# Attention setup and first value products as single pieces in the recurrences' last steps, and weighing as the last work of an attention step

## The chip, the cores and the metric

One core of one Trainium2 chip runs the whole program. The metric is the device time of one execution in microseconds (us), as the median of three runs; a further execution was taken by the hardware profiler. The engines are PE (TensorE, matrix products), DVE (VectorE), ACT (ScalarE), POOL (GpSimd) and SP (SyncE, which here only issues DMAs). Each has its own instruction stream, and they meet only at semaphores.

## The reference

Four residual layers over x of shape (8, 512, 512): batch B = 8, time T = 512, width D = 512.

```python
# layer 0: gated recurrence over time
fused = sigmoid(concat([x_t, h]) @ w_W + w_b); r, o = split(fused)
m = x_t @ wx_W + wx_b + r * (h @ wh_W + wh_b)
h = o * h + (1 - o) * tanh(m)
# layers 1 and 2: h = tanh(x_t @ Wx + b + h @ Wh)
# layer 3: causal attention, 16 heads of 32, with one more key and value, the "image" (from cond)
q, k, v = split(x @ c_attn_w + c_attn_b)
k = concat([cond @ uk_w.T + uk_b, k]); v = concat([cond @ uv_w.T + uv_b, v])
scores = where(causal, q @ k.T / sqrt(32), -10000.0) + mask
x = x + (softmax(scores) @ v) @ c_proj_w + c_proj_b
```

## The kernel before

**Three blocks in a row.** Between blocks stands a barrier of all engines that clears the semaphores (`clear_signals`). The first is the scan (`scan`) with all three recurrences as one software pipeline of 548 steps. Step n works on time n of layer 0, time n-18 of layer 1 and time n-36 of layer 2. So layer 0 ends with step 511; steps 512 to 529 hold layers 1 and 2 ("double steps" below), and steps 530 to 547 hold layer 2 alone ("single steps"). In such a step PE multiplies the last states by the recurrent weights (`main12`, L189), DVE transposes the product (L275) and adds the input part (L285), ACT takes the tanh (L238), and the next step's PE work waits for it. The input parts (`fills`, L208) of 16 times come in a few steps of every 16: in 512 to 515 and in 530 and 531 near the end. Every 16 steps DVE also adds finished states to the residual (`chunk_sum`, L321 and L323).

**The attention's setup** (`attention_setup`) is the second block. PE spreads two bias rows over partitions (L589), turns the two image weight matrices (L599, 32 transposes) and multiplies them by the condition (L605, L610); DVE and POOL keep the results and make constants. The DMAs of the attention's weights (uk, uv, proj, qkv; 6 MB) are issued in the scan, when layer 0 has ended (L156).

**The attention** (`attention`) is the third block: 128 steps, each a unit of one batch element, one group of 4 heads and one quarter of the queries (qc = 0 to 3). 16 steps make one batch element; l is the step's place in it. PE's order in step i is written out by hand: the scores of unit i (L753), two transposes of the weights of unit i-2 (L774, "rounds" into banks 4 and 5, which ACT copies out, L860), one projection job, the weighing of values for unit i-3 (`weigh`, L796 and L802), the other rounds of unit i-2 (L774, then the sums' round L779, L780), and the remaining jobs. Jobs are 128x512 products for k, q (L730), v (L719), the hidden part (L713, L715), the output projection (L736), and the turned residual rows (L726). All jobs share bank 6: a job waits until DVE has kept the job before (`product_kept`). The jobs are spread by a table: with two jobs in a step at l = 0 (k, v), 2 (hidden, rows), 5 (q, rows), 6 (proj, rows) and 9 (q, rows). Ahead of step 0 stand five products of batch element 0: k, q, v, v, v. DVE first makes the mask's parts (L976 to L1008), and only then keeps the k product (L907).

The last units' buffers for sums, maxima and shares are rings of 4 (`RING`).

Of the kernel before, what the change touches and what calls it, by code (L numbers as in the profile page):

```python
# [21 lines left out]
ALU = mybir.AluOpType  # L22
# [3 lines left out]
P = 128  # L26
B, T, D = 8, 512, 512
KC = D // P
# [50 lines left out]

def counts(per_step):  # L80
    out = [0]
    for n in range(STEPS + 1):
        out.append(out[-1] + per_step(n))
    return out
# [24 lines left out]
def scan(nc, mem, sems, a):  # L109
# [10 lines left out]
    tiles = TILES[EARLY:]  # L120

# [9 lines left out]
    with nc.Block(no_gpsimd_drain=True) as block:  # L131

        @block.sync
        def _(sp):
# [18 lines left out]

            sp.wait_ge(s.update_done, T)
            for dst, src in ((mem.uk_rows, a["uk_w"]), (mem.uv_rows, a["uv_w"]), (mem.w_proj, a["proj_w"]), (mem.w_qkv, a["qkv_w"])):
                sp.dma_start(dst[:, :, :], src.rearrange("(k p) n -> p k n", p=P)).then_inc(s.weights_in, 16)  # L156
            sp.wait_ge(s.weights_in, 64)

        @block.tensor
        def _(pe):  # L160
# [60 lines left out]

            for n in range(STEPS):
                if n < T:
                    main0(n)
                if layers_of(n):
                    main12(n)
                if fills_of(n):
                    fills(n)
                if tile_of(n) is not None:
                    turn_tile(tile_of(n))  # L230

        @block.scalar
        def _(act):
# [16 lines left out]
            for n in range(STEPS + 1):  # L250
# [15 lines left out]
                if n < T:  # L266
                    gates(n)

        @block.vector
        def _(dve):  # L270
# [92 lines left out]

            for n in range(STEPS + 1):
# [10 lines left out]
                if n < T:  # L375
                    step0(n)

# [122 lines left out]
HG = 4  # L500
HPG = 4
HD = P // HPG
QC = T // P
PER = HG * QC
UNITS = B * PER
EXTRAS = 2
FAR = 32
MASK_OUT = -10000.0
FAR_UP = 1.0e30
HIGHEST = 3.0e38  # L510
TRI = [0, 1 + P, 2 + 3 * P, 3 + 6 * P, 3 + 10 * P]
RING = 4


HEAD_START = [("k", 0), ("q", 0), ("v", 0), ("v", 1), ("v", 2)]
# [7 lines left out]
def jobs_of(i):  # L523
# [7 lines left out]
    if u + 1 < B and l in OF_NEXT:  # L531
        jobs += [(u + 1, *job) for job in OF_NEXT[l]]
# [9 lines left out]
def attention_setup(nc, mem, sems, a):  # L542


    s = sems
    ukT, uvT = mem.ukT, mem.uvT
    turns = [(rows, dst, o, k) for rows, dst in ((mem.uk_rows, ukT), (mem.uv_rows, uvT)) for k in range(KC) for o in range(KC)]
    NTURN = len(turns) // KC

    with nc.Block(no_gpsimd_drain=True) as block:  # L550

        @block.sync
        def _(sp):
            for q, src in enumerate((a["qkv_b"][2 * D:3 * D], a["proj_b"], a["uv_b"])):
                sp.dma_start(mem.row_biases[0:1, q, :], src.rearrange("(o n) -> o n", o=1)).then_inc(s.small_in, 16)

        @block.gpsimd
        def _(pool):
            nc.gpsimd.memset(mem.ones[0:1, :], 1.0).then_inc(s.ident, 1)
            nc.gpsimd.memset(mem.drop[:, :], -HIGHEST).then_inc(s.zeroed, 1)  # L560
            nc.gpsimd.memset(mem.pick[:, :, :], 0.0).then_inc(s.zeroed, 1)
            pool.wait_ge(s.zeroed, 2)


            nc.gpsimd.affine_select(out=mem.drop[:, :], in_=mem.drop[:, :],
                                    compare_op=ALU.is_ge, fill=FAR_UP, base=0,
                                    pattern=[[-1, P]], channel_multiplier=1).then_inc(s.zeroed, 1)
            for q in range(QC):
                ins = nc.gpsimd.memset(mem.pick[:, :, FAR * q + 1:FAR * q + EXTRAS * HPG:EXTRAS], 1.0)
            ins.then_inc(s.picked, 1)  # L570
            pool.wait_ge(s.picked, 1)
            nc.gpsimd.affine_select(out=mem.pick[:, :, :], in_=mem.pick[:, :, :],
                                    compare_op=ALU.is_ge, fill=0.0, base=0,
                                    pattern=[[-1, B], [0, P]], channel_multiplier=1).then_inc(s.picked, 1)
            pool.wait_ge(s.picked, 2)
            nc.gpsimd.affine_select(out=mem.pick[:, :, :], in_=mem.pick[:, :, :],
                                    compare_op=ALU.is_ge, fill=0.0, base=0,
                                    pattern=[[1, B], [0, P]], channel_multiplier=-1)
            nc.gpsimd.memset(mem.hidden_w[:, :, :], 0.0)
            nc.gpsimd.memset(mem.probs_extra[:, :, :], 0.0)  # L580
            nc.gpsimd.memset(mem.head_wide[:, :], 0.0).then_inc(s.head_wide, 1)
            nc.gpsimd.memset(mem.k_image[:, :, :, :], 0.0).then_inc(s.image_zero, 1)

        @block.tensor
        def _(pe):
            pe.wait_ge(s.ident, 1)
            pe.wait_ge(s.small_in, 48)
            for q in range(2):
                mm = pe.matmul(mem.banks[q][:, :], mem.ones[0:1, :], mem.row_biases[0:1, q, :],  # L589
                               start=True, stop=True)  # L590
            mm.then_inc(s.rows_made, 1)
            pe.wait_ge(s.head_wide, 2)
            pe.transpose(mem.banks[6][:, 0:P], mem.head_wide[:, :], mem.ident[:, :]).then_inc(s.head_turned, 1)
            for q in range(NTURN):
                if q >= 2:
                    pe.wait_ge(s.turn_kept, q - 1)
                for r in range(KC):
                    rows, dst, o, k = turns[q * KC + r]
                    mm = pe.transpose(mem.banks[2 + q % 2][:, o * P:(o + 1) * P],  # L599
                                      rows[:, o, k * P:(k + 1) * P], mem.ident[:, :])  # L600
                mm.then_inc(s.turned, 1)
            pe.wait_ge(s.turn_kept, NTURN)
            for o in range(KC):
                for k in range(KC):
                    pe.matmul(mem.banks[4][:, B * o:B * (o + 1)],  # L605
                              ukT[:, k, o * P:(o + 1) * P], mem.condT[:, k, :],
                              start=(k == 0), stop=(k == KC - 1))
            pe.matmul(mem.banks[5][0:B, :], mem.ones[0:1, 0:B], mem.row_biases[0:1, 2, :], start=True, stop=False)
            for k in range(KC):
                mm = pe.matmul(mem.banks[5][0:B, :], mem.condT[:, k, :], uvT[:, k, :],  # L610
                               start=False, stop=(k == KC - 1))
            mm.then_inc(s.image_made, 1)

        @block.vector
        def _(dve):

            dve.wait_ge(s.head_wide, 1)
            for g in range(HPG):
                mine = mem.head_wide[HD * g:HD * (g + 1), :].rearrange("p (q c) -> p q c", q=QC)
                ins = nc.vector.memset(mine[:, :, EXTRAS * g:EXTRAS * (g + 1)], 1.0)  # L620
            ins.then_inc(s.head_wide, 1)
            nc.vector.memset(mem.tail_sum[:, :, :], 0.0)
            nc.vector.memset(mem.neg_later[:, :, QC - 1:QC], HIGHEST)

            dve.wait_ge(s.head_turned, 1)
            nc.vector.tensor_copy(mem.head_block[:, :], mem.banks[6][:, 0:P])
            dve.wait_ge(s.rows_made, 1)
            for q in range(2):
                nc.vector.tensor_copy(mem.bias_tiles[:, q, :], mem.banks[q][:, :])
            for q in range(NTURN):  # L630
                dve.wait_ge(s.turned, q + 1)
                _, dst, _, k = turns[q * KC]
                nc.vector.tensor_copy(dst[:, k, :], mem.banks[2 + q % 2][:, :]).then_inc(s.turn_kept, 1)
            dve.wait_ge(s.image_made, 1)
            dve.wait_ge(s.image_zero, 1)

            for hg in range(HG):
                col = BIAS_AT["uk_b"] + hg
                nc.vector.tensor_scalar(mem.k_column[:, hg, :], mem.banks[4][:, B * hg:B * (hg + 1)],
                                        mem.biasT[:, col:col + 1], None, ALU.add)  # L640
                for g in range(HPG):
                    rows = slice(HD * g, HD * (g + 1))
                    nc.vector.tensor_scalar(mem.k_image[rows, :, hg, g], mem.banks[4][rows, B * hg:B * (hg + 1)],
                                            mem.biasT[rows, col:col + 1], None, ALU.add)
            nc.vector.tensor_copy(mem.v_rows[0:B, :], mem.banks[5][0:B, :])

            at = BIAS_AT["qkv_b"]
            nc.vector.tensor_scalar(mem.q_bias[:, :], mem.biasT[:, at:at + HG], -HD ** -0.5, None, ALU.mult)


def attention(nc, mem, sems, a, out):
# [26 lines left out]
    with nc.Block(no_gpsimd_drain=True) as block:  # L678
# [25 lines left out]
        def _(pe):  # L704
# [105 lines left out]
            for job in HEAD_START[2:]:  # L810
                product(0, *job)
            pe.wait_ge(s.image_kept, 1)
            for i in range(UNITS + 3):
# [11 lines left out]
                if i >= 3:  # L825
                    weigh(i - 3)
# [457 lines left out]
```

## Time and profile before

| | us |
|---|---|
| median of 3 runs | 3901.76 (3895.54 to 3902.09) |
| profiled execution, own time | 3889.26 |
| its span | 3887.5 |
| PE busy in the span | 3772.9 (97%) |
| DVE, ACT, POOL busy | 2362.2, 1101.2, 36.8 |

Busy time is the union of an engine's instructions. A fp32 matrix product is recorded as two instructions, so the product of one 128x512 job (4 products) shows as x8. Ends of matrix instructions are modelled, so the distance from start to start is the safer measure. The number in square brackets is idle time ahead of an instruction and what ended it. "issue" there means that the profile shows nothing that was waited for.

### The profile page before, as it was taken

The page shows a single profiled execution, that of the slowest core. Times are in us where ns is not written, and L with a number is a line of the kernel's source. Part 1 is how long each engine was busy: PE and PEld are TensorE (multiplying, and loading weights), DVE is VectorE, ACT ScalarE, POOL GpSimd, SP SyncE. Part 2 cuts the span into 40 slices and gives each one's busy share as a digit, 9 for nine tenths or more (in the row PEclk, how much of TensorE's full clock was granted, in tenths as well). Part 3 has the DMA queues.
Part 4 walks back from the last instruction along what each step waited for, and adds up shares of the span by engine and source line. Part 5 has one row for each costly group of instructions (what it writes and reads, how often), then busy time and mean ns, then how long its engine had stood idle before and what let it go on. Part 6 is the DMA issues. An engine that isn't in the chain of part 4 may idle for free. (4 is left out here: it accounts for less than half of the span.)

```text
span 3887.5 us, 170553 instructions
## 1 busy us (share of the span) xinstructions
PE 3772.9 (97%) x77572; PEld 2491.0 (64%) x77572; DVE 2362.2 (61%) x8931; ACT 1101.2 (28%) x3961; POOL 36.8 (1%) x181
## 2 busy tenths in 40 slices
PE   7999999999999999999999999999868999999998
PEld 5777666667776666677766666677534555555555
DVE  4566666666666666666666666666535666766665
ACT  2221111111111111111111111111104555655565
POOL 0000000000000000000000000000000000000000
PEclk9999999999999999999999999999979999999999
DMA  4100000000000000000000000000100000000000
GB/s 170 31 4 3 3 3 3 3 4 3 3 3 3 3 3 4 3 3 3 3 3 4 3 3 3 3 3 3 68 1 7 12 9 12 15 12 12 13 9 20
DMA packets 34249, 46.64 MB, mean 12 GB/s; under 512 B 5819, under 2 KB 22251, under 8 KB 33526
## 3 DMA queue, kind: packets, MB, share of 16 engines
q1 hardware_dynamic: 31222, 29.43, 2.4%
q8 instruction: 610, 9.99, 1.1%
q10 hardware_dynamic: 2304, 6.29, 0.4%
q14 instruction: 113, 0.93, 0.1%
HBM read 27.33 MB, written 8.39 MB: 9 GB/s over the span
## 5 line engine op out<-in xcount | busy, mean ns | idle before, releaser
L189 PE MATMUL bank<-wh,h 128*16 128x256 f32 (+1 forms) x16960 | 987.7, 374 | 32.3 <-ACT h L238 32.3
L167 PE MATMUL bank<-wh,h 128*8 128x256 f32 x16352 | 976.1, 379 | 9.0 <-DVE h L361 9.0
L189 PEld LDWEIGHTS bank<-wh,h 128*16 128x16 f32 (+1 forms) x16960 | 490.2, 97 | 339.6 <-ACT h L238 45.3
L167 PEld LDWEIGHTS bank<-wh,h 128*8 128x8 f32 x16352 | 444.8, 90 | 345.8 <-DVE h L361 20.0
L333 DVE STREAM_TRANSPOSE tp<-bank 128x256 f32<-128x256 f32 x512 | 230.2, 450 | 607.0 <-PE bank L167 605.3
L173 PE MATMUL bank<-wh,h 128*8 128x128 f32 x16352 | 540.0, 273 | 0.0
L173 PEld LDWEIGHTS bank<-wh,h 128*8 128x8 f32 x16352 | 447.1, 90 | 108.2
L243 ACT ACTIVATE gates_sb<-pre_sb 128x32 f32<-128x32 f32 x512 | 117.3, 229 | 1207.7 <-DVE pre_sb L335 1207.7
L208 PE MATMUL bank<-first,w_qkv 128*32 128x128 f32 x11904 | 393.1, 273 | 0.0
L208 PEld LDWEIGHTS bank<-first,w_qkv 128*32 128x32 f32 x11904 | 339.9, 110 | 64.3
L238 ACT ACTIVATE h<-sum 128x64 f32<-128x64 f32 (+1 forms) x530 | 135.0, 255 | 779.5 <-DVE sum L285 779.5
L275 DVE STREAM_TRANSPOSE tp<-bank 128x256 f32<-128x256 f32 (+1 forms) x530 | 233.4, 440 | 129.7 <-PE bank L189 62.5
L299 DVE TENSOR_SCALAR xw<-bank,biasT 128x128 f32<-128x128 f32 x628 | 208.1, 348 | 158.3 <-PE bank L208 124.3
L847 ACT ACTIVATE probs<-probs,neg_max 128x385 f32<-128x385 f32 (+3 forms) x512 | 280.1, 553 | 0.0
L860 ACT COPY probsT<-bank 128x512 f32<-128x512 f32 x320 | 175.0, 588 | 333.7 <-PE bank L774 333.7
L208 PE MATMUL bank<-stage,wx 128*32 128x128 f32 x8192 | 247.9, 273 | 2.2 <-issue 2.2
L208 PEld LDWEIGHTS bank<-stage,wx 128*32 128x32 f32 x8192 | 229.1, 110 | 24.8 <-issue 2.9
L730 PE MATMUL bank<-X,w_qkv 128*128 128x512 f32 x512 | 233.0, 598 | 10.0 <-PEq L100 6.5
L943 DVE CUSTOM_DVE_ANT_0 probs<-bank,addends 128x385 f32<-128x385 f32 (+3 forms) x512 | 217.8, 482 | 31.6 <-PE bank L753 30.4
L340 DVE STREAM_TRANSPOSE tp<-bank 128x128 f32<-128x128 f32 x512 | 162.3, 317 | 79.8 <-PE bank L173 74.2
L774 PE MATMUL bank<-ident,probs 128*128 128x128 f32 x1280 | 184.0, 283 | 8.0 <-ACT probs L847 6.7
L774 PEld LDWEIGHTS bank<-ident,probs 128*128 128x128 f32 x1280 | 137.4, 142 | 78.4 <-issue 55.1
(146 smaller groups left out, 3148.6 us busy)
## 6 DMA issues: line engine op xcount, KB each, us to landing
xrows<-in_x_dram SPq DMA_DIRECT2D x32, 256.0 KB, 2.9
out_dram<-X SPq DMA_DIRECT2D x32, 256.0 KB, 2.6
w_qkv<-in_L_cond_c_attn_w_dram SPq DMA_DIRECT2D x1, 3072.0 KB, 17.7
w_qkv<-in_L_cond_w_W_dram ACTq DMA_DIRECT2D x4, 512.0 KB, 7.6
wh<-in_L_cond_w_W_dram ACTq DMA_DIRECT2D x4, 512.0 KB, 13.4
wx<-in_L_cond_Wx_dram SPq DMA_DIRECT2D x2, 1024.0 KB, 7.2
wh<-in_L_cond_Wh_dram SPq DMA_DIRECT2D x2, 1024.0 KB, 10.0
mask_all<-in_mask_Bx1x1xS_ff_dram SPq DMA_DIRECT2D x8, 256.0 KB, 3.2
```

What stands on the lines that cost most here:

```text
L167: mm = pe.matmul(mem.ps0[32 * j:32 * j + B, 0:2 * P], state[:, k, :], columns_of(mem.wh0[:, k, 0:3:2, :], j), start=(k == 0), stop=(k == K ...
L173: mm = pe.matmul(mem.ps0o[32 * j:32 * j + B, 0:P], state[:, k, :], columns_of(mem.wh0[:, k, 1:2, :], j), start=(k == 0), stop=(k == KC - 1))
L189: mm = pe.matmul(mem.ps12[32 * j:32 * j + B * len(ls), P * l0:P * l1], h12[:, k, (n - 1) % HR, l0:l1, :].rearrange("p l b -> p (l b)"), co ...
L208: mm = pe.matmul(mem.fillps[n % 2][32 * j:32 * (j + 1), f * N:(f + 1) * N], mem.wx[layer][:, k, at:at + 32], rows, start=(k == 0), stop=(k ...
L275: nc.vector.transpose(mem.tp12[:, P * l0:P * l1], mem.ps12[:, P * l0:P * l1]).then_inc(s.turned12, 1)
L299: ins = nc.vector.tensor_scalar(dst, mem.fillps[n % 2][:, f * N:(f + 1) * N].rearrange("p (t b) -> p t b", b=B), mem.biasT[:, bias:bias + ...
L333: nc.vector.transpose(mem.tp0[:, 0:2 * P], mem.ps0[:, 0:2 * P]).then_inc(s.turned0, 1)
L730: mm = pe.matmul(bank[:, :], mem.w_qkv[:, k, at:at + P], mem.X[:, k, u, :], start=(k == 0), stop=(k == KC - 1))
L774: mm = pe.transpose(bank[:, x * P:(x + 1) * P], mem.probs[qc][:, g, 1 + k * P:1 + (k + 1) * P], mem.ident[:, :])
L847: nc.scalar.activation(row, row, ACT.Exp, bias=mem.neg_max[:, slot, g:g + 1], scale=-1.0, accum_out=mem.sums[:, slot, g:g + 1]).then_inc(s ...
L860: nc.scalar.copy(mem.probsT[v % 2][:, HPG * r * P:HPG * (r + 1) * P], bank[:, :]).then_inc(s.turn_kept, 1)
L943: nc.vector.tensor_tensor_reduce(out=mem.probs[qc][:, g, keys], in0=mem.banks[g][:, 0:m], in1=mem.addends[:, TRI[qc]:TRI[qc] + m], scale=1 ...
```

## The change

The setup block and its barrier are gone. Its work, and five value products (batch element 0: chunks 0, 1, 2; element 1: chunks 1, 2), are cut into 32 pieces, which `tail_plan` puts one by one behind PE's own work of steps 513 to 544. A piece is one of the four products of a v job (20 pieces), eight transposes of an image matrix (4), four small products for the image's key (4), or one of the four for the image's value (4). The table of jobs loses the same v jobs: three ahead of step 0, two at l = 14 and 15 of element 0. DVE makes the mask's parts in steps 532 to 537 (`MASK_STEP` = T + 20), and ACT copies out the turned image matrices. POOL makes its constants beside the scan. The two bias rows come spread by the DMA itself, and the qkv weights are loaded at step 496 instead of after layer 0's end; uk and uv still come at layer 0's end, proj when the image's value is made. For all this, buffers of the scan and the attention share memory, and `RING` is 3. In an attention step `weigh` now comes last.

```diff
+EARLY_V = [(0, 0), (0, 1), (0, 2), (1, 1), (1, 2)]
+def tail_plan():
+    ...
+    pieces = [[x] for x in v[:8]] + image + [[x] for x in v[8:]]
+    plan = {}
+    for n in range(T + 1, STEPS):
+        plan[n] = pieces.pop(0) if pieces else []
+        ...
 # scan, SP
+            sp.wait_ge(s.fill_done, nfill[last0])
+            load_weights(mem.w_qkv, a["qkv_w"], s.qkv_in)
             sp.wait_ge(s.update_done, T)
+            load_weights(mem.image_rows[0], a["uk_w"], s.image_in_rows[0])
+            load_weights(mem.image_rows[1], a["uv_w"], s.image_in_rows[1])
 # scan, PE
+            def early_v(u, c, k):
+                ...
+                mm = pe.matmul(mem.vps[q % 2][:, :], X[:, k, u, c * P:(c + 1) * P], mem.w_qkv[:, k, 2 * D:3 * D],
+                               start=(k == 0), stop=(k == KC - 1))
             for n in range(STEPS):
                 ...
+                tail(n)
 # scan, DVE
+                if n == MASK_STEP:
+                    ...
+                    masked(nc, mem, s, dve, 0)
+                    dve.wait_ge(s.drop_made, 1)
+                if MASK_STEP < n <= MASK_STEP + QC:
+                    ins = addends(nc, mem, n - MASK_STEP - 1)
-RING = 4
-HEAD_START = [("k", 0), ("q", 0), ("v", 0), ("v", 1), ("v", 2)]
+HEAD_START = [("k", 0), ("q", 0)]
-def attention_setup(nc, mem, sems, a):
-    ...
 # attention, PE, step i
                     for tc in (0, 1) if i == UNITS else (2, 3):
                         project(mem.banks[tc], B - 1, tc, range(HG - 1), True)
-                if i >= 3:
-                    weigh(i - 3)
                 if 2 <= i < UNITS + 2:
                     turn(i - 2, 2, None)
                 for job in jobs[1:]:
                     product(*job)
+                if i >= 3:
+                    weigh(i - 3)
```

PE's order at the scan's end, before (L189 is the recurrent product, L208 a fill; x16 is one step of it):

```order
L189 MATMUL bank<-wh,h 16x256 x16
L208 MATMUL bank<-stage,wx 32x128 x32
L189 MATMUL bank<-wh,h 16x256 x224
L189 MATMUL bank<-wh,h 8x128 x16
L208 MATMUL bank<-stage,wx 32x128 x32
```

and after, from step 515 on (L253 is the recurrent product, L272 a fill, L294 a piece of a v product, L306 eight transposes):

```order
L253 MATMUL bank<-wh,h 16x256 x16
L272 MATMUL bank<-stage,wx 32x128 x32
L294 MATMUL bank<-w_qkv,X 128x512
L253 MATMUL bank<-wh,h 16x256 x16
L294 MATMUL bank<-w_qkv,X 128x512
L253 MATMUL bank<-wh,h 16x256 x16
L294 MATMUL bank<-w_qkv,X 128x512
```

Fourteen double steps without a fill stood with nothing between them on PE; now each has one piece behind it.

PE's order in the attention step l = 6 of batch element 1, before (L736 projection, L796 and L802 weighing, L726 the rows job, L753 the next step's scores):

```order
L736 MATMUL bank<-wh 128x512 x4
L796 MATMUL bank<-probs_extra,v_extra 32x128 x4
L802 MATMUL bank<-probsT,v 32x128 x16
L726 MATMUL bank<-ident,X 128x128 x4
L753 MATMUL bank<-kT,qT 128x512 x4
```

and after (L846 projection, L836 the rows job, L906 and L912 weighing, L863 scores):

```order
L846 MATMUL bank<-wh 128x512 x4
L836 MATMUL bank<-ident,X 128x128 x4
L906 MATMUL bank<-probs_extra,v_extra 32x128 x4
L912 MATMUL bank<-probsT,v 32x128 x16
L863 MATMUL bank<-kT,qT 128x512 x4
```

The two jobs, which share a bank, now stand side by side, and the weighing stands behind both.

## Rows read from the trace of the kernel before

**Rows 1.** Windows (busy PE, PEld, DVE, ACT, POOL; clock, DMA, GB/s): last steps, setup.
```profile
2773.82:2882.00 108.18, 70.91 (x1568) 43.71 (x1559) 33.63 (x121) 9.49 (x40) 0.00 (x0) 0.90 0.17 60
2882.00:2915.65 33.65, 23.00 (x79) 11.66 (x79) 11.91 (x39) 0.00 (x0) 5.04 (x14) 0.65 0.00 0
```
**Rows 2.** Timeline of PE, last steps (start, length, engine, line, what, [idle before]).
```profile
2799.47 1.92 PE L189 MATMUL bank<-wh,h 128*16 128x256 f32 x32 [1.19 <-ACT h L238]
...
2846.69 1.06 PE L189 MATMUL bank<-wh,h 128*8 128x128 f32 x32 [0.92 <-ACT h L238]
...
2871.62 1.90 PE L189 MATMUL bank<-wh,h 128*8 128x128 f32 x32 [0.92 <-ACT h L238]
```
**Rows 3.** Timeline of PE, the attention's head.
```profile
2915.70 5.25 PE L730 MATMUL bank<-X,w_qkv 128*128 128x512 f32 x8 [6.46 <-PEq L100]
2924.01 3.70 PE L730 MATMUL bank<-X,w_qkv 128*128 128x512 f32 x8 [3.06 <-DVE kT L907]
2928.55 0.39 PE L759 MATMUL bank<-k_image,qT 128*128 128x4 f32 x2 [0.85 <-DVE qT L910]
...
2937.75 3.70 PE L719 MATMUL bank<-w_qkv,X 128*128 128x512 f32 x8 [0.78 <-DVE v L913]
2941.38 0.51 PE L753 MATMUL bank<-kT,qT 32*128 32x129 f32 x8
```
**Rows 4.** Timeline at the scan's end and the setup's start.
```profile
2880.14 1.13 DVE L323 TENSOR_TENSOR X<-stage,h 128x384 f32<-128x384 f32 x2 [0.30 <-ACT h L238]
...
2882.40 0.19 POOL L559 MEMSET ones<- 1x128 f32 x1 [2879.97 <-POOLq L100]
```
**Rows 5.** Timeline of PE, the fill of step 515.
```profile
2792.82 0.53 PE L208 MATMUL bank<-stage,wx 128*32 128x128 f32 x12 [1.67 <-issue]
```
**Rows 6.** Timeline of PE, element 0, l = 6 and 8, l = 14 and 16.
```profile
2982.29 0.93 PE L753 MATMUL bank<-kT,qT 32*128 32x385 f32 x8
...
2992.64 0.59 PE L730 MATMUL bank<-X,w_qkv 128*128 128x512 f32 x1
...
3031.38 0.93 PE L753 MATMUL bank<-kT,qT 32*128 32x385 f32 x8
...
3045.78 0.59 PE L730 MATMUL bank<-X,w_qkv 128*128 128x512 f32 x1
```
**Rows 7.** Waits of PE in the attention (total us, times, longest us).
```profile
PE bank L779 <- issue: 7.0, 14, 0.5
PE bank L736 <- DVE wh L1035: 3.9, 8, 0.8
...
PE bank L719 <- DVE kT L907: 0.9, 1, 0.9
PE bank L796 <- ACT shareT L870: 0.6, 1, 0.6
```
**Rows 8.** Timeline of PE and DVE, element 1, from l = 6 to the next scores.
```profile
3097.50 0.43 PE L796 MATMUL bank<-probs_extra,v_extra 128*32 128x128 f32 x8
3097.61 0.69 DVE L923 TENSOR_TENSOR X<-bank,X 128x512 f32<-128x512 f32 x1 [1.49 <-PE bank L736]
...
3098.73 0.66 PE L726 MATMUL bank<-ident,X 128*128 128x128 f32 x4
3099.32 1.14 PE L753 MATMUL bank<-kT,qT 32*128 32x512 f32 x8
```
**Rows 9.** Timeline of PE, job against weighing, and job against transposes.
```profile
3101.32 3.60 PE L736 MATMUL bank<-wh 128*128 128x512 f32 x8
3104.84 0.42 PE L796 MATMUL bank<-probs_extra,v_extra 128*32 128x128 f32 x8
...
3857.05 2.74 PE L736 MATMUL bank<-wh 128*128 128x512 f32 x6
3859.63 1.05 PE L740 MATMUL bank<-ident,X 128*128 128x128 f32 x8
```
**Rows 10.** Timeline of POOL beside a DVE addition.
```profile
3856.01 0.56 POOL L1061 COPY extras<-probs 128x4 f32<-128x4 f32 x1 [4.21 <-ACT probs L847]
```

More of the change, by code:

```diff
@@ L77, in sum_of @@
     return None
+HG = 4
+HPG = 4
+HD = P // HPG
+QC = T // P
+PER = HG * QC
+UNITS = B * PER
+EXTRAS = 2
+FAR = 32
+MASK_OUT = -10000.0
+FAR_UP = 1.0e30
+HIGHEST = 3.0e38
+TRI = [0, 1 + P, 2 + 3 * P, 3 + 6 * P, 3 + 10 * P]
+RING = 3
+MASK_STEP = T + 20
+EARLY_V = [(0, 0), (0, 1), (0, 2), (1, 1), (1, 2)]
+def tail_plan():
+    v = [("v", u, c, k) for u, c in EARLY_V for k in range(KC)]
+    image = [[("turn", 0, 0), ("turn", 0, 1)], [("turn", 0, 2), ("turn", 0, 3)]]
+    image += [[("k", o)] for o in range(KC)]
+    image += [[("turn", 1, 0), ("turn", 1, 1)], [("turn", 1, 2), ("turn", 1, 3)]]
+    image += [[("image", k)] for k in range(KC)]
+    pieces = [[x] for x in v[:8]] + image + [[x] for x in v[8:]]
+    plan = {}
+    for n in range(T + 1, STEPS):
+        plan[n] = pieces.pop(0) if pieces else []
+        if n >= T + LAG12[0] and len(layers_of(n)) == 1 and pieces and pieces[0][0][0] != "k":
+            plan[n] = plan[n] + (pieces.pop(0) if len(pieces) > STEPS - 1 - n else [])
+    assert not pieces
+    return plan
+TAIL = tail_plan()
 def counts(per_step):
@@ L267, in _ @@
                     gates(n)
+                for _, w, k in tail_of(n - 1, "turn"):
+                    q = KC * w + k
+                    act.wait_ge(s.turned, q + 1)
+                    if w:
+                        act.wait_ge(s.image_k_made, KC)
+                    nc.scalar.copy(mem.image_T[:, k, :], mem.xps[q % 2][:, :]).then_inc(s.turn_kept, 1)
         @block.vector
@@ L531, in jobs_of @@
     if u + 1 < B and l in OF_NEXT:
-        jobs += [(u + 1, *job) for job in OF_NEXT[l]]
+        jobs += [(u + 1, *job) for job in OF_NEXT[l] if job[0] != "v" or (u + 1, job[1]) not in EARLY_V]
     if u and l in ROWS_OF_LAST:
@@ L539, in unit @@
     return i // PER, i % PER // QC, i % QC
-def attention_setup(nc, mem, sems, a):
[L545 to L648, printed above, removed]
@@ L1019, in _ @@
             hidden_weights(0)
-            for job in HEAD_START[2:]:
-                keep(0, *job)
-            hidden_extreme(0)
             for i in range(UNITS + 3):
@@ L1146, in __init__ @@
         self.x_in = [new(f"x_in{q}") for q in range(4)]
+        self.once = len(self.all)
+        self.mask_in = new("mask_in")
+        self.mask_made = new("mask_made")
+        self.mask_used = new("mask_used")
+        self.masked_ready = new("masked_ready")
+        self.extreme = new("extreme")
+        self.tail_summed = new("tail_summed")
+        self.hidden_exp = new("hidden_exp")
 def build(nc, a, out):
@@ L1160, in build @@
         assert nums == list(range(nums[0], nums[0] + len(nums)))
-        mem.sem_range = range(nums[0], nums[-1] + 1)
+        mem.sem_range = range(nums[0], nums[sems.once])
         banks = [bank(f"bank{q}") for q in range(8)]
@@ new lines, in build @@
+        mem.neg_far = sums[:, 0:T]
+        mem.replacing = sums[:, T:2 * T].rearrange("p (k c) -> p k c", k=QC)
+        wx1 = sb(ctx, "wx1", [P, KC * D])
+        mem.addends = wx1[:, 0:TRI[-1]]
+        mem.mask_all = wx1[:, TRI[-1]:TRI[-1] + T]
+        at = TRI[-1] + T
+        mem.mask_col, mem.far_col, mem.neg_inside = (wx1[:, at + QC * q:at + QC * (q + 1)] for q in range(3))
+        at += 3 * QC
+        mem.neg_later, mem.later_max, mem.neg_hidden, mem.tail_sum = (
+            wx1[:, at + 2 * QC * q:at + 2 * QC * (q + 1)].rearrange("p (u k) -> p u k", u=2) for q in range(4))
@@ L1200, in build @@
             mem.sum12 = sb(part, "sum12", [P, 2, KC, B])
-            mem.first = sb(part, "first", [P, KC, N])
-            mem.xrows = sb(part, "xrows", [P, XR, D])
             with ExitStack() as load:
```

307 lines of the change are left out of this document (203 added, 104 removed).

## The prediction

> **What bounds the kernel now.** I read the busy line, then windows by stage, then PE's timeline. PE is busy for 97% of the span, so the question is where it is not. Two stretches stand out [rows 1]: the last steps of the scan, from layer 0's end, where PE works 70.91 of 108.18 us, and the setup block, with 23.00 of 33.65 us at a granted clock of 0.65. In the last steps PE waits for its own result to come round over DVE and ACT: each double step is 1.92 us of work behind 1.19 idle (3.11 us), each single step 1.06 behind 0.92 (1.98) [rows 2]. [...] In the attention PE is the bound, with a few waits of known size (term 5).
>
> Durations are those of the profiled execution (3889.3 us). The median is 3901.8, which is 12.5 above it. I subtract from the one and carry the difference to the other.
>
> **Term 1, the last steps (+0.2 us).** A piece of a v product is one of four such products; four take 3.70 + 0.78 = 4.48 us from one start to the next [rows 3], of which 0.97 is the wait for DVE's keep (term 5), so a piece is 0.88 us at most, and 0.86 without a change of shape (term 5). A double step has 1.19 us free and a single step 0.92, so by these rows nearly all pieces fit; I add 0.1 us to 10 single steps for what spills, 1.0 us. The eight transposes of a piece take about 1.0 us beside 1.19. Five steps hold a fill too (513 to 515, 530, 531), and there PE has no idle time: 5 x 0.86 = 4.3 us in full. DVE's mask work in step 532 I estimate at 2 us, behind a residual addition of 1.1 us like the one in [rows 4]. That is more than the 1.98 us of a single step leaves, and step 537 has a v keep and the last reduction together: 1.3 + 0.5 = 1.8 us. Against this: the fill of step 515 lost 1.67 us to "issue" [rows 5] while 6 MB of weights were arriving. With qkv loaded 16 steps earlier the burst is split; I take back 1.2 us. And with pieces in every step the clock should not fall: seven steps had the long product, the first only in part, and their excess over 1.98 sums to 5.7 us. 1.0 + 4.3 + 1.8 - 1.2 - 5.7 = +0.2. Bounds: if no single step is long and nothing spills, -3; if the clock falls as before and each of 30 pieces spills 0.2 us, +12.
>
> The ACT copies (two per turn piece, about 0.6 us each) stand between two tanhs that are over 2.8 us apart. The POOL constants are off the path.
>
> **Term 2, setup block and head (-49.2 us).** Before, from the scan's last DVE instruction (2880.14 + 1.13 = 2881.27, [rows 4]) to the first scores (2941.38, [rows 3]) it is 60.1 us. After: one barrier (2882.40 - 2881.27 = 1.13, [rows 4]), the k product with its keep, the q product with its keep (2928.55 - 2924.01 = 4.54, [rows 3]; k takes 0.1 more for one extra small copy, 4.6), and the image product with its ACT copy, which I put at 0.65. 1.13 + 4.6 + 4.54 + 0.65 = 10.9 us. Gone are the setup, a barrier, the 3.06 us in which the q product waited because DVE made the mask ahead of the k keep, the slow clock of the first product (5.25 instead of 3.70), and three v products with their keeps of 4.48 us each. What is late next: ACT's table load and hidden exponentials begin at once, since the mask is ready, and end before the image copy. If the head starts at the low clock, add 1.2 us. A second small gain: k's second product no longer waits for the last v keep, 0.4 us (**term 3**).
>
> **Term 4, two steps without v (-4.0 us).** Element 0, l = 14 and 15, lose a 3.5 us job each, but then DVE and ACT set the pace. Element 0 already has the same pair without jobs at l = 6 and 7. From the scores of l = 6 to the job of l = 8 it is 2992.64 - 2982.29 = 10.35 us, from l = 14 to 16 it is 3045.78 - 3031.38 = 14.40 [rows 6]. The difference is 4.05. The bounds are 7 (both jobs in full) and 1.5, because DVE has a mask job in each of these two steps.
>
> **Term 5, weighing last (-3.2 us).** Three things happen in the 7 elements that have a predecessor.
> - Two jobs that share bank 6 now stand side by side at l = 2 and l = 6. The second must wait for the keep of the first: PE was free for the next work at 3097.50, and that keep ends at 3097.61 + 0.69 = 3098.30 [rows 8]; with the way to PE 0.97 us. Before, weighing covered it. 14 x 0.97 = +13.6 us. At l = 0 the v job stands behind only 0.7 us of transposes after the k job, whose keep costs about 1.05 (the wait of 0.9 in [rows 7] is this pair with nothing between): 7 x 0.35 = +2.5 us.
> - Waits that go: the rows job stands ahead of the weighing at l = 5 and 9, so DVE keeps it about 1 us earlier and makes the next shares earlier. The wait of 0.5 us, 14 times, is this one: the profile calls it "issue", but DVE's reciprocal ends just there. -7.0 us. The wait for wh at l = 3 goes for the same reason: its row has 3.9 us in 8 waits, the longest, 0.8, at the very end, so 7 are left with -3.1 us.
> - A change of array shape costs PE some time. The job to weighing takes 3104.84 - 3101.32 = 3.52 us for eight records, while six records to full transposes take 3859.63 - 3857.05 = 2.58 us, 0.43 each, which makes 3.44 for eight [rows 9]. So a switch is about 0.1 us, and weighing next to the scores saves one. 92 steps have it: 7 x 12, where nothing waits, and 8 in element 0. -9.2 us.
> 13.6 + 2.5 - 7.0 - 3.1 - 9.2 = -3.2. The bounds are +6 (no switch is saved) and -17 (the side-by-side jobs cost nothing).
>
> The wait in front of the sums' round at qc = 3 stays, since it stands behind the same transposes. Rings of 3 cost nothing: DVE then waits for the transposes of unit i-3, which PE has passed before it starts the scores that DVE needs anyway.
>
> **Term 6, the end (-1.4 us).** The last weighing waited 0.6 us for ACT's copy of the sums [rows 7]; with the weighing before it moved behind the transposes, this and some 0.8 us of similar waits are covered.
>
> **Sum.** +0.2 - 49.2 - 0.4 - 4.0 - 3.2 - 1.4 = -58.0. The profiled execution would be 3831.3 us, the median 3843.8; I say 3844.
>
> [...] POOL's one wait at an end is 0.56 us for a copy that takes 0.19, beside a DVE addition of two SBUF tensors [rows 10]: here POOL was held. [...] No row here shows DVE held, so it stays a rival at 3 in 100.
>
> **The rivals.**
> - [...] Chance 12%.
> - The pieces are not hidden: PE takes the state's weights only when the piece is through, so every piece costs its own time. Against it: the fill in a double step costs PE only what exceeds the loop. Price: 27 more pieces at 0.86 = 23 us: 3867. Chance 6%.
> - Weighing last goes badly only in size: waits at l = 0, 2, 6 as computed, but no switch is saved: 3844 + 9 = 3853. Chance 9%. The other way, the side-by-side jobs cheap: 3830, chance 5%.
> - Slower than before: the rounds of transposes, no longer parted by weighing, find their bank uncopied in every step. A wait for DVE in that place was at most 0.8 us [rows 7]. 96 steps at 0.8 would be 77 us and give 3921. It decides from 0.6 us a step (58 / 96). Against it: in all but a few steps a job of 3.5 us stands between the first two rounds and the others. Chance 2%.
> - The POOL rival above: 3%.
>
> **How the numbers follow.** The forecast has the other 63%, with its own range from 3834 to 3852. The rivals at 3853 and 3830 take the range to 3828 and 3858, which leaves out the unhidden pieces, the slower case and a part of the offset between profiled and timed runs. Less than 0.2% (8 us) can't be told from no change here. All cases but one are beyond it: faster 0.97, same 0.01, slower 0.02.
>
> **What would show it.** The profile after should have no setup block, about 11 us from the scan's last DVE instruction to the first scores, a clock at full level to the scan's end, and single steps of 2.0 us with a piece in each. In the attention there should be a new wait of PE, 14 times about 0.8 us, for DVE's keep of the hidden part and of the projection, in front of the rows job, while the 14 "issue" waits of 0.5 are gone. I am wrong if single steps come near 2.8 us, if those waits are missing, or if the attention's steady steps are longer by more than 0.1 us.

## The result and the profile after

| | before | after |
|---|---|---|
| median | 3898.73 us (4 runs, 3895.54 to 3902.09) | 3827.09 us (4 runs, 3823.46 to 3828.67) |
| ratio | | 0.9822, 95% interval 0.9809 to 0.9834 |
| profiled execution, own time | 3889.26 | 3826.17 |
| its span | 3887.5 | 3824.5 |
| PE busy in the span | 3772.9 (97%) | 3746.8 (98%) |

The change is faster, as forecast, and by more: 71.6 us between the medians where 58 were forecast. In microseconds 3827.09 lies just below the range (3828 to 3858). As a ratio to the kernel before, whose median over four runs is 3 us lower than over three, it lies inside: 0.9822, where the range's lower end is 3828 / 3901.76 = 0.9811. The two spans are 63.0 us apart: 47.5 from the scan's last DVE instruction to the first scores, 1.1 in the last steps (103.56 us against 104.67 for the same 36 steps), 15.4 from the first scores to the end, and 1.0 lost again in the earlier scan. Of this 1.0, 0.9 is there by step 34, where both kernels do the same work; the last 0.1 comes at step 497, behind the earlier load of the qkv weights.

Windows after (length, then busy us of PE, PEld, DVE, ACT, POOL; granted clock as a share of full speed, DMA share, GB/s): the last steps, then the head.

```profile
2777.59:2881.15 103.56, 95.14 (x1648) 53.63 (x1648) 40.26 (x142) 12.57 (x44) 3.92 (x14) 1.00 0.10 32
2881.15:2893.80 12.65, 9.46 (x19) 3.75 (x19) 1.78 (x6) 3.81 (x11) 0.00 (x0) 0.87 0.09 23
```

Against [rows 1]: the clock is 1.00 where it was 0.90, PE works 95 of 104 us, and the setup block of 33.65 us is gone.

Timeline of PE after, in the last steps: a fill step with its piece, a double step, and two single steps.

```profile
2792.10 1.93 PE L272 MATMUL bank<-stage,wx 128*32 128x128 f32 x64
2793.96 1.12 PE L294 MATMUL bank<-w_qkv,X 128*128 128x512 f32 x2
2795.02 1.92 PE L253 MATMUL bank<-wh,h 128*16 128x256 f32 x32
2796.87 1.13 PE L294 MATMUL bank<-w_qkv,X 128*128 128x512 f32 x2
2798.13 1.92 PE L253 MATMUL bank<-wh,h 128*16 128x256 f32 x32
...
2863.77 1.06 PE L253 MATMUL bank<-wh,h 128*8 128x128 f32 x32
2864.76 1.13 PE L294 MATMUL bank<-w_qkv,X 128*128 128x512 f32 x2
2865.81 1.06 PE L253 MATMUL bank<-wh,h 128*8 128x128 f32 x32
```

The double step keeps its 3.11 us (2795.02 to 2798.13) with a piece in it, the single step takes 2.04 (1.98 in [rows 2]), and the product stays at 1.06 to the end of the scan, where [rows 2] has 1.90. The granted clock is 1.00 in the last 22 us of the scan here; in the profile before it is 1.00 from 2846.69 to 2857.50 us and 0.50 from 2861.50 to 2881, where a single step takes 2.82 us instead of 1.98.

Timeline of the head after, answering to [rows 3, 4].

```profile
2880.01 1.14 DVE L443 TENSOR_TENSOR X<-stage,h 128x384 f32<-128x384 f32 x2 [0.29 <-ACT h L352]
2882.34 5.37 PE L840 MATMUL bank<-X,w_qkv 128*128 128x512 f32 x8 [3.24 <-PEq L140]
2888.61 3.70 PE L840 MATMUL bank<-X,w_qkv 128*128 128x512 f32 x8 [0.91 <-DVE kT L1015]
...
2893.16 0.39 PE L869 MATMUL bank<-k_image,qT 128*128 128x4 f32 x2 [0.84 <-DVE qT L1018]
...
2893.80 0.50 PE L863 MATMUL bank<-kT,qT 32*128 32x129 f32 x8 [0.25 <-ACT wx L995]
```

Between barrier, k, q and image product nothing else is left. The k product, behind 3.24 us of idleness at the barrier, takes 5.37 us instead of 3.70; its granted clock is 0.68, that of the q product 1.00.

Waits of PE in the attention after (total us, times, longest), answering to [rows 7].

```profile
PE bank L889 <- ACT probsT L968: 9.8, 37, 1.0
PE bank L884 <- ACT probs L955: 6.6, 7, 2.1
PE bank L836 <- DVE v_extra L1023: 5.5, 7, 0.8
PE bank L836 <- DVE X L1031: 5.5, 7, 0.8
PE bank L829 <- DVE kT L1015: 2.9, 8, 0.9
PE bank L846 <- DVE wh L1102: 0.8, 1, 0.8
```

The 14 forecast waits of the rows job (L836) are there with 0.8 us each, and seven at l = 0 (L829, about 0.3 each). The 14 "issue" waits are gone, and of the wait for wh (L846) one of 0.8 is left. In element 1, l = 6, which answers to [rows 8]:

```profile
3038.32 3.68 PE L846 MATMUL bank<-wh 128*128 128x512 f32 x8
...
3042.04 0.69 DVE L1031 TENSOR_TENSOR X<-bank,X 128x512 f32<-128x512 f32 x1 [1.48 <-PE bank L846]
3042.79 0.66 PE L836 MATMUL bank<-ident,X 128*128 128x128 f32 x4 [0.79 <-DVE X L1031]
```

From the projection's start to the next work it is 4.47 us, where it was 3.61 (3093.89 to 3097.50): the side-by-side pair costs 0.86.

### The profile page after: what moved, and what is told of

It reads as the page before. It is cut to its first block and busy times, and to the rows that moved or that the text cites. A ratio compares the mean times of both kernels' runs of the same rounds, so it can differ in the third digit from the quotient of the medians.

```text
span 3824.5 us, 170528 instructions
## 1 busy us (share of the span) xinstructions
PE 3746.8 (98%) x77565; PEld 2492.1 (65%) x77565; DVE 2358.2 (62%) x8897; ACT 1104.8 (29%) x3969; POOL 39.6 (1%) x192
## 5 line engine op out<-in xcount | busy, mean ns | idle before, releaser
L253 PE MATMUL bank<-wh,h 128*16 128x256 f32 (+1 forms) x16960 | 982.6, 372 | 7.6 <-ACT h L352 6.9
L231 PE MATMUL bank<-wh,states 128*8 128x256 f32 x16352 | 976.1, 379 | 9.4 <-DVE states L481 9.4
L253 PEld LDWEIGHTS bank<-wh,h 128*16 128x16 f32 (+1 forms) x16960 | 487.0, 96 | 321.6 <-ACT h L352 25.1
L231 PEld LDWEIGHTS bank<-wh,states 128*8 128x8 f32 x16352 | 445.1, 90 | 346.1 <-DVE states L481 20.5
L237 PE MATMUL bank<-wh,states 128*8 128x128 f32 x16352 | 540.0, 273 | 0.0
L237 PEld LDWEIGHTS bank<-wh,states 128*8 128x8 f32 x16352 | 447.2, 90 | 108.1
L357 ACT ACTIVATE gates_sb<-pre_sb 128x32 f32<-128x32 f32 x512 | 117.5, 229 | 1207.9 <-DVE pre_sb L455 1207.9
L272 PE MATMUL bank<-probs_extra,w_qkv 128*32 128x128 f32 x11904 | 393.1, 273 | 0.0
L272 PEld LDWEIGHTS bank<-probs_extra,w_qkv 128*32 128x32 f32 x11904 | 339.9, 110 | 64.3
L1051 DVE CUSTOM_DVE_ANT_0 probs<-bank,wx 128x385 f32<-128x385 f32 (+3 forms) x512 | 218.9, 484 | 34.7 <-PE bank L863 33.4
L359 ACT ACTIVATE gates_sb<-pre_sb 128x32 f32<-128x32 f32 x512 | 117.4, 229 | 240.2 <-DVE pre_sb L462 240.2
L405 DVE TENSOR_TENSOR sum<-tp,xw 128x32 f32<-128x32 f32 x1024 | 152.0, 188 | 18.2
L840 PEld LDWEIGHTS bank<-X,w_qkv 128*128 128x128 f32 x512 | 92.8, 191 | 98.8 <-issue 96.4
```

The lines of the kernel that those rows point to most:

```text
L231: mm = pe.matmul(mem.ps0[32 * j:32 * j + B, 0:2 * P], state[:, k, :], columns_of(mem.wh0[:, k, 0:3:2, :], j), start=(k == 0), stop=(k == K ...
L237: mm = pe.matmul(mem.ps0o[32 * j:32 * j + B, 0:P], state[:, k, :], columns_of(mem.wh0[:, k, 1:2, :], j), start=(k == 0), stop=(k == KC - 1))
L253: mm = pe.matmul(mem.ps12[32 * j:32 * j + B * len(ls), P * l0:P * l1], h12[:, k, (n - 1) % HR, l0:l1, :].rearrange("p l b -> p (l b)"), co ...
L272: mm = pe.matmul(mem.fillps[n % 2][32 * j:32 * (j + 1), f * N:(f + 1) * N], mem.wx[layer][:, k, at:at + 32], rows, start=(k == 0), stop=(k ...
L840: mm = pe.matmul(bank[:, :], mem.w_qkv[:, k, at:at + P], mem.X[:, k, u, :], start=(k == 0), stop=(k == KC - 1))
L1051: nc.vector.tensor_tensor_reduce(out=mem.probs[qc][:, g, keys], in0=mem.banks[g][:, 0:m], in1=mem.addends[:, TRI[qc]:TRI[qc] + m], scale=1 ...
```

## The experiments

Times are medians; each kernel is compared with runs of the kernel before on the same chip (medians 3894.24, 3895.17 and 3895.47 in the three groups; the changed kernel's ratio of 0.9822 makes about 3825 to 3826 there). "e" is the time of one full batch element in the attention, from the scores of a step to those of the same step 16 later: 117.19 us before, 115.53 after, within 0.02 us in each element from the third on (in the second, l = 0 can be longer). It is the sharpest measure here.

**1. Weighing back in its old place.**

```diff
+                if i >= 3:
+                    weigh(i - 3)
                 if 2 <= i < UNITS + 2:
                     turn(i - 2, 2, None)
                 for job in jobs[1:]:
                     product(*job)
-                if i >= 3:
-                    weigh(i - 3)
```

> The changed kernel with the weighing of unit i-3 back in its old place, behind the first job; the scan, the setup's pieces and the head stay as changed. Theory (the attention gained 15.4 us by the two traces, of which 3.45 + about 1 are the two steps without v and the end, so the order of the weighing carries 9 to 11): about 3837, so 0.984 to 0.985 of the kernel before; each plain attention step 0.14 to 0.15 longer than in the changed kernel, the 14 issue waits of 0.5 us at the sums' round back, the 14 waits of the rows job gone. My forecast's size (term 5, -3.2, and the end, -1.4) would give 3831 to 3832. Rival (the order of the weighing is worth nothing, and the attention's gain comes from where its data lie and from rings of 3): 3827.

Measured: 3841.25, ratio 0.9864 (0.9851 to 0.9877); e = 117.19, exactly that of before; the "issue" waits are back (7.0 us, 14). So the order alone makes the difference in e, and neither the rings of 3 nor where data lie has a part in it. The loss, 14 us by the medians and 16 by the ratios, is more than 7 x 1.66 = 11.6 and more than the 9 to 11 expected; two stretches of 20 us early in the attention have a clock of 0.83 and 0.91 in this profile, where the changed kernel has 1.00. Why the clock dips there is open.

**2. Weighing last, alone, in the kernel before.**

```diff
-                if i >= 3:
-                    weigh(i - 3)
                 ...
                 for job in jobs[1:]:
                     product(*job)
+                if i >= 3:
+                    weigh(i - 3)
```

> The kernel before with one edit: the weighing of unit i-3 comes last in a step. Theory: -9 to -11 us against the kernel before (each of some 92 plain steps 0.14 shorter = -13; 14 side-by-side jobs cost 0.86 each = +12; 14 gone waits of 0.7 = -10 and 7 of about 0.4; l = 0 adds some 0.2 x 7), so a ratio of 0.9972 to 0.9977. By the terms as forecast (-3.2 and -1.4) it would be -4.6, 0.9988. Rival (worth nothing alone): 1.000.

Measured: 3883.41, ratio 0.9966 (0.9954 to 0.9979), 10.8 us less; e = 115.52. From first scores to end it is 936.41 us against 946.12: 9.7 of the 15.4. The forecast's 4.6 (terms 5 and 6, ratio 0.9988) lies outside the interval, and e shows why (below).

**3. Weighing between the side-by-side jobs.**

```diff
+                split = i < UNITS and i % PER in (0, 2, 6)
+                if i >= 3 and split and i % PER:
+                    weigh(i - 3)
                 if 2 <= i < UNITS + 2:
                     turn(i - 2, 2, None)
+                if i >= 3 and split and not i % PER:
+                    weigh(i - 3)
                 for job in jobs[1:]:
                     product(*job)
-                if i >= 3:
+                if i >= 3 and not split:
                     weigh(i - 3)
```

> The changed kernel, but in the steps where two jobs of one bank stand side by side (l = 2 and 6) the weighing stands between them again, and at l = 0 between the transposes and the v job. Theory (there the second job waits 0.86 us from start to start for the first one's keep, 14 times, and 0.3 more at l = 0, 7 times; the two extra changes of array shape cost 0.15 each): 3827 - 12 - 1 + 2 = about 3816, ratio 0.9788. Rival (a wait removed there turns up at the next place, since DVE's keeps and the shares run behind as before): 3825 to 3827, ratio 0.981 to 0.982.

Measured: 3816.71, ratio 0.98 (0.9787 to 0.9812, which just touches the changed kernel's 0.9809 to 0.9834); e = 114.19, 1.34 less than after. Its waits of PE:

```profile
PE bank L889 <- ACT probsT L973: 10.4, 37, 1.5
PE bank L884 <- ACT probs L960: 6.6, 7, 2.1
PE bank L846 <- DVE wh L1107: 3.9, 8, 0.8
```

The rows job waits no more. The wait for wh of 3.9 us is back (7 of 0.44), so a part does turn up again, but 7 x 1.34 = 9.4 us stay. A cover that the change had taken away was worth having in 3 steps of 16.

**4. The weighing split.** The small products of the weighing (L906) move ahead of the second pair of transposes; the others stay last.

```diff
                 ...
+                if i >= 3:
+                    weigh_extra(i - 3)
                 if 2 <= i < UNITS + 2:
                     turn(i - 2, 2, None)
                 ...
```

> The changed kernel with the small first part of the weighing (the product with the image's value, four products 32 wide) moved alone ahead of the second pair of transposes; nothing else moves. It adds changes of array shape to each of 126 steps but no wait for data. Theory (a change of shape costs PE time, 0.1 to 0.15 us, and that is what each plain step gained when weighing moved next to the scores): 0.1 to 0.2 a step, +12 to +25 us, 3840 to 3852, ratio 0.985 to 0.988. Rival (a change of shape is free, and the plain steps are shorter since something else overlaps better): 3827, ratio 0.982.

Measured: 3846.81, ratio 0.9879 (0.9866 to 0.9892); e = 118.05, or 2.52 more, 0.29 in a plain step (6.63 against 6.34 us). The expected 0.1 to 0.2 a step was too low. The same small groups in three orders: on their own between job and transposes (this run); in the changed kernel, where the job stands next to the transposes; and in the kernel before, with all the weighing between them:

```profile
3148.36 3.60 PE L840 MATMUL bank<-X,w_qkv 128*128 128x512 f32 x8
3151.89 0.42 PE L906 MATMUL bank<-probs_extra,v_extra 128*32 128x128 f32 x8
3152.25 0.66 PE L884 MATMUL bank<-ident,probs 128*128 128x128 f32 x4
3152.74 0.27 PE L889 MATMUL bank<-ident,shares 128*128 128x128 f32 x1
```

```profile
3139.06 3.60 PE L840 MATMUL bank<-X,w_qkv 128*128 128x512 f32 x8
3142.49 0.60 PE L884 MATMUL bank<-ident,probs 128*128 128x128 f32 x4
3142.93 0.27 PE L889 MATMUL bank<-ident,shares 128*128 128x128 f32 x1
3143.04 0.27 PE L890 MATMUL bank<-ident,extras 128*8 128x128 f32 x1
3143.24 0.42 PE L906 MATMUL bank<-probs_extra,v_extra 128*32 128x128 f32 x8
3143.49 0.62 PE L912 MATMUL bank<-probsT,v 128*32 128x128 f32 x16
```

```profile
3546.87 3.60 PE L730 MATMUL bank<-X,w_qkv 128*128 128x512 f32 x8
3550.40 0.43 PE L796 MATMUL bank<-probs_extra,v_extra 128*32 128x128 f32 x8
3550.64 0.62 PE L802 MATMUL bank<-probsT,v 128*32 128x128 f32 x16
3551.20 0.66 PE L774 MATMUL bank<-ident,probs 128*128 128x128 f32 x4
3551.69 0.27 PE L779 MATMUL bank<-ident,shares 128*128 128x128 f32 x1
```

From start to start, the job takes 3.53 us before the narrow products and 3.43 before transposes. The narrow group takes 0.36 before transposes and 0.24 or 0.25 before its own kind; the transposes behind narrow products take 0.49 instead of 0.44. No data are waited for in any of these rows. So a change of shape cost time on both sides here: 0.10 and 0.05 where all the weighing moved (0.15 a step), and 0.14 more here, most of it (0.11) in the small group that stands apart.

**5. An idle product in the gaps, kernel before.** Nothing is moved; the product's result is read by nobody.

```diff
+                if len(layers_of(n)) == 1 and n > T and n < STEPS - 1:
+                    pe.matmul(mem.banks[3][:, :], mem.wx[1][:, 0, 0:P], mem.wx[2][:, 0, :], start=True, stop=True)
```

> The kernel before with one idle product (128x512, its result is read by nobody) added on PE behind its own work in each of the single steps 530 to 546; all the work stays where it was. Theory (the granted clock falls in the single steps because PE is idle for 0.92 of each 1.98 us; work in the gap holds it, and costs 0.07 a step and 1.17 in each of the two fill steps): single products of 1.06 us to the end, steps of 2.05. Against the profiled execution of before (seven long steps, 5.7 us) that is -2 to -3 us; against executions whose clock fells at step 534 or 536, as in the last two profiled executions of kernels with the same scan, -7 to -8; so -2 to -8 in the median, 0.998 to 0.9995, and a narrower spread. Rival (the clock falls whatever PE does there, or each product adds its 0.86 us): no gain, or +15 us (1.004).

Measured: 3888.36 (12 runs), ratio 0.9982 (0.9974 to 0.9991): 7.1 us less than its own group of runs before (0.9982 x 3895.47), by adding work. Its single steps:

```profile
2863.83 1.06 PE L189 MATMUL bank<-wh,h 128*8 128x128 f32 x32
2864.82 1.13 PE L232 MATMUL bank<-wx 128*128 128x512 f32 x2
2865.88 1.06 PE L189 MATMUL bank<-wh,h 128*8 128x128 f32 x32
```

The product is 1.06 us to the end, the step 2.05, as in the changed kernel, and the granted clock is 1.00 from 2845 to 2881 us. No other work was moved, so it is the work in the gaps that held the clock.

**6. Two early value products instead of five.**

```diff
-EARLY_V = [(0, 0), (0, 1), (0, 2), (1, 1), (1, 2)]
+EARLY_V = [(0, 0), (0, 1)]
-HEAD_START = [("k", 0), ("q", 0)]
+HEAD_START = [("k", 0), ("q", 0), ("v", 2)]
 ... (PE makes and DVE keeps the third job behind the image product)
```

> The changed kernel with only two of the five value products made early: 12 pieces stand in the last steps instead of 20 beside those of the image, so most single steps are empty again; one v product stands in the head and two at l = 14 and 15 of element 0 again. Theory (the pieces in the single steps are what holds the clock): the last single products take 1.9 us again and a step 2.8 instead of 2.05, +5.7 us less the 0.06 that each piece costs, +5 in all; with +4.5 in the head, 3827 + 13.. The two steps with v again cost 3.45: 3840, ratio 0.985. Rival (the clock would be kept without the pieces, since no barrier follows): 3835, and single products of 1.06 us to the end.

Measured: 3843.71, ratio 0.9868 (0.9853 to 0.9883), where 3840 was expected. The pieces end in step 532, and the granted clock falls at once, to 0.50 from 2851 to 2888 us:

```profile
2848.80 1.06 PE L253 MATMUL bank<-wh,h 128*8 128x128 f32 x32 [1.61 <-ACT h L352]
2850.78 1.63 PE L253 MATMUL bank<-wh,h 128*8 128x128 f32 x32 [0.93 <-ACT h L352]
2853.32 1.90 PE L253 MATMUL bank<-wh,h 128*8 128x128 f32 x32 [0.91 <-ACT h L352]
...
2887.30 1.89 PE L253 MATMUL bank<-wh,h 128*8 128x128 f32 x32 [0.99 <-ACT h L352]
```

The steps from 534 on are long (2.5, then 2.8 us), 14 of them and not the last seven: twice the price that I had taken from one profile. With experiment 5 this settles that the pieces in the gaps keep the clock in this kernel.

**7. Fewer pieces in fill steps** (3 of 32 instead of 5; the others one per step elsewhere).

```diff
-    for n in range(T + 1, STEPS):
+    slots = [n for n in range(T + 1, STEPS - 1) if not fills_of(n)]
+    slots = [T + 1, T + 2, T + 3][3 - (len(pieces) - len(slots)):] + slots if len(pieces) > len(slots) else slots
+    for n in slots:
         ... (a rule for leftover pieces is taken out)
```

> The changed kernel with other places for the pieces: 3 of 32 instead of 5 stand in steps with a fill, the others in steps without. Theory (a fill step has no idle time, so a piece there costs its whole 1.17 us from start to start, and a piece elsewhere 0.06 at most): -2.3 us, 3825. If pieces cost the same everywhere: 3827.

Measured: 3826.09, ratio 0.9821 (0.9804 to 0.9837); not told apart from the changed kernel. Step 530 became 0.85 us shorter (2.55 instead of 3.40), but in this profile PE was idle for 2.44 us behind the mask step, the clock stood at 0.72 from 2848 to 2854 us, and the next two steps took 2.22 and 3.18 us. Step 531, freed as well, gave only 0.03, since DVE's mask work behind it sets the pace. Experiment 10 has the same plan of pieces and the same idle time (2.46 us) without the dip: there the last 36 steps are 1.3 us shorter than in experiment 3. So the expected 2.3 was too much in any case.

**8. Rings of 3 in the kernel before** (`RING = 3`).

> The kernel before with rings of 3 buffers for sums, maxima and shares instead of 4. Theory (DVE would wait for transposes that PE has long passed): no change, 1.000. Rival (data lie elsewhere or ACT and DVE wait for one another): -3 to +8 us, 0.999 to 1.002.

Measured: 3894.83 (10 runs), ratio 1.0001 (0.9992 to 1.0011); e = 117.18. No change, as expected.

**9. The qkv load 16 steps earlier, kernel before** (one execution, read for its fill steps only).

```diff
             ... (load_late issues one of the loads)
+            sp.wait_ge(s.fill_done, nfill[T - CH])
+            load_late(mem.w_qkv, a["qkv_w"])
             sp.wait_ge(s.update_done, T)
-            for dst, src in ((mem.uk_rows, a["uk_w"]), (mem.uv_rows, a["uv_w"]), (mem.w_proj, a["proj_w"]), (mem.w_qkv, a["qkv_w"])):
+            for dst, src in ((mem.uk_rows, a["uk_w"]), (mem.uv_rows, a["uv_w"]), (mem.w_proj, a["proj_w"])):
             ...
```

> The kernel before, but the qkv weights (3 MB of the 6 MB that are loaded when layer 0 has ended) are asked for 16 steps earlier, as in the changed kernel; no piece is moved. The steps 513 to 515 with fills take 3.54, 4.27 and 5.37 us in the profiled execution of before, and 3.55, 4.28 and 5.90 in that of the kernel with the weighing last, where nothing but a halt of PE for no shown reason makes them longer than 3.47. Theory (PE's halts come from the burst of 6 MB): all three at 3.5, -2.7 us, and at most a small halt at steps 497 to 499. Rival (they come from something else that begins when layer 0 ends): still one of 1 us or more.

Measured: the steps 514 and 515 are 4.17 and 3.47 us, instead of 4.27 and 5.37 ([rows 5]) and, in the profile of experiment 2, 5.90. The large halt is gone, the small one of about 0.7 us stays, so the expected 3.5 for all three did not come out in full. It is one execution, but the large halt is in all four profiles with the old load (before, experiments 2, 5 and 8) and in none of the seven others with the new one. Its own time in this one execution, 3899.2, tells nothing of 2 us: 14 single steps were long in it.

**10. Experiments 3 and 7 together.** The edits are those shown.

> The changed kernel with both: the weighing between the two side-by-side jobs at l = 2 and 6 (and in its old place between transposes and job at l = 0), and the pieces kept out of the fill steps. If both gains add: 3816.7 - 2.3 = 3814.4, ratio about 0.979.

Measured: 3815.83, ratio 0.9797 (0.9782 to 0.9811). e is 114.19 again. Faster than the kernel before and, by e, than the changed kernel (the two intervals of the ratio touch); not told apart from experiment 3 alone (3816.71).

## Why the prediction was right, and where it missed

The sign and the main mechanisms of the forecast were right (setup gone, pieces hidden, clock held, order of the weighing); the sizes were not, and the gain at the end (term 6) did not come. 3844 was forecast, 17 more than measured. 5 of the 17 are in the profiled executions (3831.3 forecast, 3826.2 measured), 12 in what I added on top. The 5 are themselves a sum of larger misses of both signs, in part by luck, as the terms show.

- **The carry from the profiled execution to the median (12.5 us, now 0.9): the larger miss.** I took the difference as a property of the kernel that the change would keep. It was a property of this one execution: among 45 timed runs of the kernel before in four groups (median 3895.47) a single one is below the 3889.3 of the profiled one. Seven single steps were long in it, while profiles of kernels with the same scan have 12 (experiment 8), 14 (2) and 14 (9), each 0.83 us more. The median of the 45 is also 6.3 below the 3901.76 of the first three, so half of the 12.5 was chance in those. Most of the other half is, I think, the varying clock in the scan's last steps (seven more long steps are 5.8 us), which the change removes, and with it the offset. No run shows this split.
- **Term 1 (+0.2; measured -1.1).** Double steps hide a piece wholly (3.11 us with it). Single steps pay 0.06 (forecast 0.1). A piece in a fill step costs 4.64 - 3.47 = 1.17, not 0.86: from the fill's start to the piece's it is 1.86 us, where it was 1.75 to the next state product, and the piece then takes 1.05. Against this, the issue halts were 0.8 and 1.9 us in the profile before and both are gone, 2.7 where I took back 1.2. Steps 530 to 532, with two pieces and the mask work, became 2.5 longer, step 537 0.5. The granted clock stayed at 1.00, and the 5.7 of the seven long steps (up to 2.82 us each, where the profile before has 0.50) came back as forecast.
- **Term 2 (-49.2; measured -47.5).** Off by the slow first product (5.37 instead of 3.70, 1.67 us, at a granted clock of 0.68), which the prediction had named as a risk of 1.2 and left out of the sum.
- **Term 3 (-0.4; measured -0.4).** From the first scores to the second it is 8.67 us, where it was 9.09.
- **Term 4 (-4.0; measured -3.45).** From the scores of l = 14 to the job of l = 16 it is now 10.95 us instead of 14.40. Nearly right.
- **Term 5 (-3.2; with term 6, the order alone -9.7 in the trace of experiment 2).** Here the sum failed. For one element I had -0.46, e says -1.66. The side-by-side pairs cost 2 x 0.86 (forecast 0.97), and l = 0 0.5 (forecast 0.35): good enough. The waits that went gave more than their idle time. The "issue" wait of 0.5, before and after:

```profile
3561.12 0.66 PE L774 MATMUL bank<-ident,probs 128*128 128x128 f32 x4
3562.28 0.30 PE L779 MATMUL bank<-ident,shares 128*128 128x128 f32 x1 [0.50 <-issue]
3562.41 0.27 PE L780 MATMUL bank<-ident,extras 128*8 128x128 f32 x1
```

```profile
3037.47 0.66 PE L884 MATMUL bank<-ident,probs 128*128 128x128 f32 x4
3037.96 0.27 PE L889 MATMUL bank<-ident,shares 128*128 128x128 f32 x1
3038.07 0.27 PE L890 MATMUL bank<-ident,extras 128*8 128x128 f32 x1
```

  From L774 to L780 it was 1.29 us and is 0.60: 0.69 for each of the two in an element (forecast 0.5). The wait for wh gave 0.68 (forecast 0.44). The largest miss is "a switch is about 0.1 us": [rows 9] give only the way from the wide to the narrow shape. The way back cost 0.05 in the next group of transposes, which I did not look for. A plain step is 0.15 shorter (6.49 to 6.34). 12 of an element's 16 steps gain it, as many as forecast; in l = 2, 6, 10 and 14 no transposes stand behind the job, so the weighing has nothing to move behind. Together 1.72 + 0.5 - 1.38 - 0.68 - 1.8 = -1.64, against the -1.66 of e.
- **Term 6 (-1.4; not seen).** The last weighing's wait of 0.6 us is gone, but from the scores of the last element's l = 11 to the end it is 59.4 us at a clock of 0.91, where it was 56.6 at 0.97. In experiment 2, where only the order differs, it is 56.7 at 0.96: nothing gained. So the 15.4 us from the first scores to the end hold dips of the clock of both signs: this one against the change, and one of about 2 us in its favour, since the profile before has a clock of 0.83 in element 0, l = 4 (10.14 us, 8.15 after).

The rivals: a clock that falls in the single steps or pieces that spill (12 in 100), and the pieces not hidden, are refuted by the single steps of 2.04 at a granted clock of 1.00 and the double steps of 3.11. The bank left uncopied in every step does not exist: the plain steps became shorter. "Side-by-side jobs cheap" (3830) came nearest in time, but for a wrong reason, since they cost 0.86. POOL beside the scan cost nothing worth a microsecond: its eight selects stand at 2778.91 to 2781.68, and at 2780.05 the two DVE additions among them took 0.34 us instead of 0.29. That POOL's constants could hold DVE there was my supposition, which no row of before showed; POOL's moved work is 5.04 us in [rows 1], and the additions beside its selects are 0.05 longer.

## What to carry to other kernels

A gap in which an engine waits for its own result was room for independent work in pieces that fit (a double step stayed at 3.11 us with a piece, a single step went from 1.98 to 2.04), and on PE the filling was worth more than its own time here, where the clock had been falling in the gaps: 17 idle products made the kernel 7.1 us shorter (experiment 5). Before carrying an offset from one profiled execution to a median, ask what in that execution varies from run to run and whether the change removes it. When an order is changed, count changes of shape both ways (0.10 and 0.05 us here), and put a covering group back just where two jobs share a buffer.

## What the runs showed of the hardware

- The granted clock fell from 1.00 to 0.50 of full speed in step 541 of the profile before (a single product went from 1.06 to 1.90 us), though PE had not been idle for more than 0.93 us at a time in the eight steps of 1.98 ahead of it. In profiles of other kernels with the same scan it fell in step 534 or 536. One idle product in each gap (1.06 us from its start to the next product's) held it at 1.00 (experiment 5).
- In the attention it also fell behind short idle times, in some profiles and not in others. In experiment 10, l = 0 of element 1 follows waits of 0.61, 0.29 and 0.56 us, the granted clock is 0.60 from 2986.45 to 2990.68 us and 0.68 in its job, which takes 5.33 us instead of 3.60:

```profile
2986.45 2.54 PE L863 MATMUL bank<-kT,qT 32*128 32x129 f32 x8 [0.56 <-DVE minima L1056]
2988.91 1.97 PE L884 MATMUL bank<-ident,probs 128*128 128x128 f32 x8
2990.68 5.33 PE L840 MATMUL bank<-X,w_qkv 128*128 128x512 f32 x8
```

  Experiment 3 has nearly the same waits there (0.60, 0.29, 0.56), a granted clock of 1.00 and a job of 3.60. What decides is open.
- Two changes of array shape between products 128 and 32 wide cost 0.15 us where the weighing moved (a plain step of 6.49 against 6.34). One more narrow group of eight records on its own made a plain step 0.29 longer (experiment 4).
- A wait of PE cost more than the idle time that the profile shows: removing 0.50 us idle gave 0.69 from start to start, removing 0.44 gave 0.68.
- PE halted for 1.66 to 2.22 us with nothing to wait for while 6 MB of weights were loading (four profiles); with 3 MB asked for 16 steps earlier the long halt was gone (experiment 9 and seven profiles of changed kernels).
